# Layer 2's routed rows return inside the program of the blocks: Pool sums the pairs, and layer 3's values follow the last block on TensorE

## The reference, cut to what matters

```python
def _L2_ffn_ref(x, w12, w3, shared_w1, shared_w2, shared_w3, router_w, expert_bias):
    shared = jax.nn.silu(xf @ shared_w1.T) * (xf @ shared_w2.T) @ shared_w3.T
    scores = jax.nn.sigmoid(xf @ router_w.T)
    _, top_idx = jax.lax.top_k(scores + expert_bias, TOP_K)
...
    h = jax.nn.silu(h1) * h2 * gates[:, :, None]
    routed = jnp.einsum('teh,edh->td', h, w3)
    return (shared + routed).reshape(b, s, d)

def _L3_xattn_ref(hidden_states, hidden_states_multi, Wg, Wq, Wk, Wv, Wo, W1, b1, W2, b2):
...
    v = jnp.einsum('bsh,hd->bsd', xm, Wv)
    attn = jax.nn.softmax(jnp.einsum('bqd,bkd->bqk', q, k) * scale, axis=-1)
    e0 = jnp.einsum('bqk,bkd->bqd', attn, v) @ Wo
...
x = x + _L2_ffn_ref(_layernorm(x, axis=-1), ...)
x = x + _L3_xattn_ref(_layernorm(x, axis=-1), ctx_1024, ...)
```

## Time and profile before

| what | value |
|---|---|
| median of 3 runs | 1523.82 us (1521.71 to 1527.78) |
| the profiled execution | 1522.15 us, span of its trace 1520.2 us |
| TensorE busy | 1398.9 us, 92% of the span |
| VectorE, ScalarE, Pool busy | 896.2, 692.9, 355.8 us |
| mean granted clock of TensorE | 0.949 |

### The profile page before, as it was taken

How to read it: one execution, slowest core, us unless ns; L and a number is a source line. 1 busy time by engine, 2 the same in 40 slices (tenths; PEclk the granted TensorE clock), 3 DMA queues, 4 the chain that set the end, 5 groups by cost and what they waited for, 6 DMA issues and landing times. The chain is left out here.

```text
span 1520.2 us, 24680 instructions
## 1 busy us (share of the span) xinstructions
PE 1398.9 (92%) x8362; PEld 1123.9 (74%) x8362; DVE 896.2 (59%) x1703; ACT 692.9 (46%) x1133; POOL 355.8 (23%) x367
## 2 busy tenths in 40 slices
PE   5799999799999999999999699999989888996894
PEld 4544444588888889888888677888867776885783
DVE  6778887745555455555545753444455657654555
ACT  5356667343443344344333265555543254452431
POOL 2102223311222122122211022333310046531100
PEclk8889999889999999999999899999999979998896
DMA  6802120111111111111110024555521143332000
GB/s 224 258 8 58 47 70 16 55 38 62 41 41 59 44 41 41 62 41 41 53 50 7 20 69 104 142 145 144 139 84 70 42 130 125 111 98 76 29 1 28
DMA packets 63799, 110.83 MB, mean 73 GB/s; under 512 B 10331, under 2 KB 39517, under 8 KB 62845
## 3 DMA queue, kind: packets, MB, share of 16 engines
q1 hardware_dynamic: 61869, 104.93, 23.4%
q0 software_dynamic: 1872, 5.13, 0.9%
HBM read 90.91 MB, written 18.97 MB: 72 GB/s over the span
## 5 line engine op out<-in xcount | busy, mean ns | idle before, releaser
L1217 DVE TENSOR_TENSOR hidden_l<-silu_l,up_l 128x512 f32<-128x512 f32 x128 | 88.0, 688 | 220.3 <-ACT silu_l L1157 220.3
L1157 ACT ACTIVATE silu_l<-gate_l 128x512 f32<-128x512 f32 x128 | 76.5, 598 | 308.6 <-PE up_l L75 308.6
L851 DVE TENSOR_REDUCE maxima<-a_scores 128x1 f32<-128x512 f32 x256 | 164.6, 686 | 41.5 <-PE a_scores L790 40.1
L818 ACT ACTIVATE probs<-b_scores 128x1024 f32<-128x1024 f32 x128 | 131.0, 1023 | 67.1 <-PE b_scores L747 65.1
L75 PE MATMUL out_l<-dn_hi_l,h_lo_l 128*128 128x256 f32 x512 | 144.9, 283 | 0.0
L74 PE MATMUL out_l<-dn_lo_l,h_hi_l 128*128 128x256 f32 x512 | 144.9, 283 | 0.0
L73 PE MATMUL out_l<-dn_hi_l,h_hi_l 128*128 128x256 f32 x512 | 144.7, 283 | 0.0
L1189 POOL TENSOR_TENSOR gu_lo_l<-gu_raw_l,gu_hi_l 128x1024 fp32r<-128x1024 f32 x31 | 74.2, 2393 | 299.1 <-ACT gu_hi_l L1149 299.1
L1241 DVE SCALAR_TENSOR_TENSOR x_sb<-out_l,cw,x_sb 128x256 f32<-128x256 f32 x256 | 109.0, 477 | 22.4 <-PE out_l L75 18.1
L1223 DVE TENSOR_TENSOR h_lo_l<-hidden_l,h_hi_l 128x512 fp32r<-128x512 f32 x128 | 102.2, 798 | 3.2
L73 PE MATMUL gate_l<-xnT_hi_n,gu_hi_l 128*128 128x512 f32 x256 | 101.3, 396 | 1.0 <-DVE xnT_lo_n L191 1.0
(11 more groups left out here) (487 smaller groups left out, 3564.1 us busy)
## 6 DMA issues: line engine op xcount, KB each, us to landing
gu_raw_l<-w_units SPq DMA_DIRECT2D x32, 512.0 KB, 3.7
spread_l<-cw_rows SPq DMA_DIRECT2D x64, 256.0 KB, 3.9
dn_raw_l<-w_units SPq DMA_DIRECT2D x32, 256.0 KB, 2.6
k_stack<-k_stacks SPq DMA_DIRECT2D x8, 768.0 KB, 5.7
staged_l<-w_experts SPq DMA_DIRECT2D x24, 256.0 KB, 2.7
up_raw_l<-w SPq DMA_DIRECT2D x40, 128.5 KB, 3.4
dn_raw_l<-w SPq DMA_DIRECT2D x40, 128.0 KB, 2.0
phi_a<-fside SPq DMA_DIRECT2D x8, 512.0 KB, 3.3
```

The source lines that it names most:

```text
L818: act.activation(probs[u % 4][:, :, :], b_scores[:, u % 2, :, :], ACT.Exp, scale=SCALE).then_inc(exp_done, 1)
L851: dve.tensor_reduce(maxima[k // 16][:, i // 2, i % 2:i % 2 + 1], a_scores[:, k % 2, :], X, ALU.max).then_inc(a_read, 1)
L1157: act.activation(silu[:, q % 2, :], gate[:, q % 2, :], ACT.Silu).then_inc(silu_done, 1)
L1217: dve.tensor_tensor(hidden[:, q % 2, :], silu[:, q % 2, :], up[:, q % 2, :], ALU.mult).then_inc(hidden_done, 1)
```

## The change

The program `l2_return_phase` is gone, and its work stands at the end of `l2_sparse_phase`, ahead of that program's one barrier.

- TensorE's list goes on behind the last block with `wvo` and the eight value tiles. `wvo` lies in bank 0 of `gate`; the value tiles use eight places in PSUM that the blocks and the shared expert used (`value_banks`), with a wait for the last block's result ahead of the seventh tile.
- The halves of `wvo` go into `dn_hi` and `dn_lo`, two instructions of 128x256 for one of 128x512, on ScalarE and on VectorE.
- SyncE waits for the blocks' loads to be used up and for all scatters, then loads the four pairs into buffers that are free by then (`staged`, `gu_raw`, `hidden`, `dn_raw`). `dn_raw` becomes one buffer of two halves for that.
- Pool sums the pairs, behind its last scatter. VectorE only adds the sum to `g.x`; a round takes the statistics of the chunks before.

```diff
-        gu_raw, dn_raw = several("gu_raw", [P, 2, KC, FS]), several("dn_raw", [P, D])
+        gu_raw, dn_raw = several("gu_raw", [P, 2, KC, FS]), sb("dn_raw", [P, 2, D])
...
+        spare = [staged[i][:, :, :] for i in range(RING)]
...
+        parts = [spare[2 * i:2 * i + 2] for i in range(PIECE)]
+        wvo = gate[:, 0, :]
+        value_banks = [gate[:, 1, :], up[:, 0, :], up[:, 1, :], banks[:, 0, :], banks[:, 1, :], gate[:, 0, :], banks[:, 2, :], banks[:, 3, :]]
...
             def _(sp):
...
+                sp.wait_ge(pair_split, 2)
+                for i in range(OUTS):
+                    sp.wait_ge(scattered[i], 16 * len(range(i, NB2, OUTS)))
+                for i in range(PIECE):
+                    for w in range(2):
+                        at = w * T + 2 * i * P
+                        sp.dma_start(parts[i][w], g.routed[at:at + 2 * P, :].rearrange("(c p) e -> p c e", p=P)).then_inc(part_loaded[i], 16)
...
             def _(pe):
...
+                pe.wait_ge(pair_split, 2)
+                pe.wait_ge(x_hi_done, NB2)
+                pe.wait_ge(x_lo_done, NB2)
+                for c in range(KC):
...
+                last.then_inc(wvo_done, 1)
+                pe.wait_ge(wvo_hi_done, KC)
+                pe.wait_ge(wvo_lo_done, KC)
...
+                for m in range(VALUES):
+                    if m == 6:
+                        pe.wait_ge(result_done, NB2)
...
             def _(act):
...
+                act.wait_ge(wvo_done, 1)
+                for k in range(KC):
+                    act.activation(dn_hi[k][:, :], wvo[:, k * D:(k + 1) * D], ACT.Copy).then_inc(wvo_hi_done, 1)
...
             def _(pool):
...
+                for i in range(PIECE):
+                    pool.wait_ge(part_loaded[i], 32)
+                    pool.tensor_tensor(parts[i][0], parts[i][0], parts[i][1], ALU.add).then_inc(summed, 1)
+                    pool.wait_ge(summed, i + 1)
...
             def _(dve):
...
+                for m in range(VALUES - LATE):
+                    value_low(m)
+                for i in range(PIECE):
+                    add_routed(i)
+                    if i >= 1:
+                        take_stats(dve, g, (2 * i - 2, 2 * i - 1))
+                    value_low(VALUES - LATE + i)
+                    dve.wait_ge(returned, i + 1)
+                take_stats(dve, g, (TC - 2, TC - 1))
...
-        l2_return_phase(nc, g)
```

More of the change, by code:

```diff
@@ L2170, in l2_sparse_phase, with v_of @@
         g.pair_hi, g.pair_lo = [g.v_hi[:, 8 + 4 * i:12 + 4 * i, :].rearrange("p (w k) f -> p w k f", w=2) for i in range(2)]
-        g.scattered2 = [(scattered[i], 16 * len(range(i, NB2, OUTS))) for i in range(OUTS)]
+        PIECE, VALUES = TC // 2, CT // P // 2
+        spare = [staged[i][:, :, :] for i in range(RING)]
+        spare += [gu_raw[i][:, :, :, :].rearrange("p w k f -> p (w k f)").rearrange("p (c e) -> p c e", c=2) for i in range(2)]
+        spare += [hidden[:, i, :].rearrange("p (c e) -> p c e", c=2) for i in range(2)] + [dn_raw[:, :, :]]
+        parts = [spare[2 * i:2 * i + 2] for i in range(PIECE)]
+        part_loaded, summed, returned = [sem(f"part_loaded{i}") for i in range(PIECE)], sem("parts_summed"), sem("parts_added")
+        wvo = gate[:, 0, :]
+        value_banks = [gate[:, 1, :], up[:, 0, :], up[:, 1, :], banks[:, 0, :], banks[:, 1, :], gate[:, 0, :], banks[:, 2, :], banks[:, 3, :]]
+        wvo_done, wvo_hi_done, wvo_lo_done = sem("wvo3_done"), sem("wvo3_hi_done"), sem("wvo3_lo_done")
+        values_done, v_hi_done, v_lo_done = sem("v3_done"), sem("v3_hi_done"), sem("v3_lo_done")
+        def v_of(half, m):
+            return half[:, 2 * m:2 * m + 2, :].rearrange("p c e -> p (c e)")
         pair_loaded, pair_split = sem("pair_loaded"), sem("pair_split")
@@ L2342, in _ @@
                         block_down(step - 3, experts.pop(step - 3))
+                pe.wait_ge(pair_split, 2)
+                pe.wait_ge(x_hi_done, NB2)
+                pe.wait_ge(x_lo_done, NB2)
+                for c in range(KC):
+                    f = slice(c * P, (c + 1) * P)
+                    for k in range(KC):
+                        last = mm3(pe, wvo[:, c * D:(c + 1) * D], (g.pair_hi[:, 0, k, f], g.pair_lo[:, 0, k, f]),
+                                   (g.pair_hi[:, 1, k, :], g.pair_lo[:, 1, k, :]), c == 0 and k == 0, k == KC - 1)
+                last.then_inc(wvo_done, 1)
+                pe.wait_ge(wvo_hi_done, KC)
+                pe.wait_ge(wvo_lo_done, KC)
+                pe.wait_ge(b_silu_done, NB2)
+                pe.wait_ge(b_hidden_done, NB2)
+                for m in range(VALUES):
+                    if m == 6:
+                        pe.wait_ge(result_done, NB2)
+                    for j in range(2):
+                        t = slice((2 * m + j) * P, (2 * m + j + 1) * P)
+                        for k in range(KC):
+                            last = mm3(pe, value_banks[m][:, j * D:(j + 1) * D], (g.ctxT_hi[:, k, t], g.ctxT_lo[:, k, t]),
+                                       (dn_hi[k][:, :], dn_lo[k][:, :]), j == 0 and k == 0, k == KC - 1)
+                    last.then_inc(values_done, 1)
             @block.scalar
@@ L2355, in split_dn @@
                         act.wait_ge(down_done, 2 * (n - DEPTH + 1))
[L2356 removed]
+                    act.activation(dn_hi[n % DEPTH][:, :], dn_raw[:, n % DEPTH, :], ACT.Copy).then_inc(dn_hi_done, 1)
                 def split_piece(i):
@@ L2421, in _ @@
                         act.activation(result[b % OUTS], y_bank[b % 2][:, 0:D], ACT.Copy, scale=s.weight[:, b:b + 1]).then_inc(result_done, 1)
+                act.wait_ge(wvo_done, 1)
+                for k in range(KC):
+                    act.activation(dn_hi[k][:, :], wvo[:, k * D:(k + 1) * D], ACT.Copy).then_inc(wvo_hi_done, 1)
+                for m in range(VALUES):
+                    act.wait_ge(values_done, m + 1)
+                    act.activation(v_of(g.v_hi, m), value_banks[m], ACT.Copy).then_inc(v_hi_done, 1)
             @block.gpsimd
@@ L2541, in _ @@
                         dve.tensor_tensor(flat(b_lo[b % 2]), h_bank[b % 2][:, 0:D], f32(flat(b_hi[b % 2])), ALU.subtract).then_inc(b_lo_done, 1)
[L2544 to L2604, removed]
-                    dve.wait_ge(v_hi_done, m + 1)
[L2606 to L2614, removed]
@@ L2623, in _ @@
[L2623 to L2627, removed]
-                for i in range(PIECE):
[L2629 to L2632, removed]
+                    dve.tensor_tensor(g.x[:, chunks, :], g.x[:, chunks, :], parts[i][0], ALU.add).then_inc(returned, 1)
@@ new lines, in _ @@
+                for k in range(KC):
+                    dve.wait_ge(wvo_hi_done, KC)
+                    dve.tensor_tensor(dn_lo[k][:, :], wvo[:, k * D:(k + 1) * D], f32(dn_hi[k][:, :]), ALU.subtract).then_inc(wvo_lo_done, 1)
+                LATE = PIECE
+                for m in range(VALUES - LATE):
+                    value_low(m)
+                for i in range(PIECE):
+                    add_routed(i)
[3 more added lines that the diff above has]
+                    dve.wait_ge(returned, i + 1)
```

14 lines of the change are left out of this document (8 added, 6 removed).

## The result

The changed kernel takes 1515.2 us (median of 5 runs, 1512.4 to 1518.34) against 1523.82: a ratio of 0.9942, 95% interval 0.9924 to 0.996. In a second comparison (first experiment) it was 1511.28 against 1523.48, 0.9914, interval 0.9899 to 0.9929. It is faster, by 6 to 15 us. Runs of one kernel differ by up to 6 (the change) and 8 us (before), so what each part is worth is read from one stretch of the traces, from the last block to the last statistics, which repeats within 0.6 us.

A forecast was written before the change was run, and what follows sets the result against it. In the stretch, a barrier waiting for Pool's DRAIN bounds first, then TensorE, then VectorE. Terms -6.0 - 1.3 + 0.1 - 1.95 - 1.7 = -10.85 us gave 1511.3 or 1513.0, stated as 1512.0; range 1509 to 1517.

The forecast's parts named there:

- The barrier goes: Ahead of `wvo` on TensorE: it starts at 1375.5 instead of 1381.52, behind the last block's matmuls, saving 6.0 us.
- The clock: `wvo` on TensorE: matmuls at 2.4 GHz take 1.42 us and a tail of 0.2 instead of 2.9, saving 1.3.
- Both rivals on the clock behind `wvo`: Clock falls in the gap and returns: 1513.4 us, chance 0.09; stays low for all eight value tiles: 1520.3, chance 0.05.
- Halves in two pieces: `wvo`'s halves on ScalarE and VectorE: two 128x256 instructions each instead of one 128x512, costing 0.1 us, at worst 0.33.
- First four value tiles: From first value matmul until VectorE reaches its first routed work: 7.1 us instead of 9.05, saving 1.95.
- VectorE's loop: VectorE's four rounds without the sums: 7.7 us undisturbed, 8.7 with held-up adds, instead of 10.41, saving 1.7.
- The 1.0 for the lock: VectorE's first three routed adds each meet a running Pool sum on the shared port, together 1.0 us later.
- the rival without that: VectorE's routed adds are not held up or loads come sooner: 1.0 us more saved, 1510.3 to 1512, chance 0.09.
- Ready?: Pairs land at about 1383, 1385, 1387 and 1389, so each Pool sum is there before VectorE wants it.
- What is left at the end: Barrier behind VectorE's last statistics: Pool's DRAIN adds 0 us, and layer 3's front starts at the same clock.
- a sign that it is wrong: Listed sign against the forecast: layer 3's front takes longer than before.
- Slower, by the clock of layer 3's front: Clock recovery in layer 3's front slips: by 11 us all saving is gone, by 20 us 1531; chance 0.04.

The follow-up runs named there:

- first experiment: The changed kernel and the kernel before, both unaltered, run once more: 1511.28 us against 1523.48, ratio 0.9914; stretch 19.89 us against 30.21.
- two experiments: Kernel before with pairs' sums moved to Pool, barrier kept: loop 7.71 us, ratio 0.9982. Changed kernel loading pairs from input x: loop 7.72 us, ratio 0.9927.
- second profile: Profile of the unaltered changed kernel's repeat run: stretch 19.89 us, VectorE's loop 9.38, layer 3's front 30.5; ratio to the kernel before 0.9914.
- pairs from the input: Changed kernel, but SyncE loads the eight pieces from input x without waiting for the scatters, leaving routed rows out: stretch 18.23 us, ratio 0.9927.

## Why the prediction was right, and which terms were off

The forecast of 1512.0, faster, with 1509 to 1517, holds both medians, 1515.2 and 1511.28, and the mechanism is the one described. That the second median comes so near is in part chance: it lies 12.2 us below the kernel before, and the stretch accounts for 9.7 to 10.3. By its steps, with the first profile of after:

- *The barrier goes*, -6.0: right. No wait ahead of `wvo`.
- *The clock*, -1.3: right. `wvo` to its copy took 1.64 for 1.62 forecast, at 1.00, and the pause of 1.58 ahead of the values left the clock up. Both rivals on the clock behind `wvo` are out.
- *Halves in two pieces*, +0.1: from copy to first value 1.55 instead of 1.47.
- *First four value tiles*: 7.3 instead of the 7.1 forecast.
- *VectorE's loop*, -1.7: **the step that was mis-sized.** It gave 0.6 and 1.0 in the two profiles. The 7.7 us for an undisturbed loop were right to 0.02 (two experiments). The 1.0 for the lock was as measured, 1.09, though it came from one add held up fully, not three by parts; in every profile of this kernel one add is held up, so the rival without that is out. What failed is "Ready?": "I put the pairs at about 1383, 1385, 1387 and 1389". SyncE's load came 2.6 us behind the last scatter for 2.8 forecast, but the first pair was there 4.9 us behind that load (4.3 in the second profile), not 3.2. I had taken the shortest of the eight landings, 2.7, and an issue; but a pair is two loads, and behind the old barrier too the first was there only after 3.8 and the second after 6.25 (the run with Pool's sums in the kernel before). The landings themselves did not get slower: the median of the eight is 4.5 and 4.6 in the two profiles, 5.0 before. In the first profile the issue of the first pair was 0.9 longer, so its second pair came after 7.1, against 6.2 in the second profile. What lengthened that issue, and why the first pair took 4.3 and not 3.8 in the second profile, was not tried. So VectorE waits 0.88 for the second sum, and 0.43 in the second profile.
- *What is left at the end*: the DRAIN "I take 0, by the 47 ns" was wrong, since the program of that row issues no DMA on Pool. It takes 3.24 us, from 1393.1 to 1396.3, and costs nothing only because VectorE ends 0.9 later; in the forecast's own times it would have ended some 0.8 ahead of VectorE (1390.3 + 0.2 + 3.2 against 1394.5, an estimate). So the sum stands, but not for the reason given. "I take the same start" of the front: it took as long in one profile, and 1.3 us longer in the other, which the prediction had named as a sign that it is wrong.
- *Slower, by the clock of layer 3's front*: the front was 1.3 longer at most, not 11. The clock came back 8.4 to 8.5 us behind the barrier in the two profiles of before, 8.3 and 11.5 us in those of the change; the front with 11.5 is the one with the later weights, so how much of the 1.3 is the clock stays open.

The sum, -10.85, measured -9.7 and -10.3; by steps, in the first profile, -6.15 - 1.29 + 0.08 - 1.76 - 0.60 = -9.72.

The rule of the Trainium skill on the shared port (SBUF — State Buffer, section on the two separate sides) said that Pool would wait for adds as well, which no row of before showed: the third sum's 1.76 shows it. The other rule of the Trainium skill, which gives elementwise adds to VectorE (GPSIMD Engine Reference, Engine selection), leads to the version without Pool's sums. The prediction put that at 9.2; it measured 9.2 to 9.3, and Pool's sums still brought 0.5 to 1.0.

## What to carry to other kernels

A barrier behind DMAs that Pool issued can cost more than the transfers (here Pool's DRAIN ended 4.2 us behind the start of the last scatter, while SyncE could load the scattered rows 2.6 us behind it), so move work across it that needs none of them, and count the DMAs. Work moved to Pool was worth its full time, 2.7 us, only where it was done before VectorE's adds of two SBUF operands began; where they met, late sums and held-up adds left 0.5 to 1.0 of it. And a step that needs two loads comes with the later of them, so price it by the median landing, not by the shortest.

## What the runs showed of the hardware

- Pool's DRAIN at the end of a program took 40 ns and 82 to 89 ns more for each DMA that Pool had issued in it: 129, 701 and 3235 ns for 1, 8 and 39. They were 3235 whether the DRAIN began 6.6 us behind the last scatter's start (pairs from the input) or 14.5 (the change).
- Pool's two-operand instruction held up VectorE's normalisation too, which reads one tensor: 4.54 us instead of 2.67 beside 2.34 us of Pool. The Trainium skill (SBUF — State Buffer, Who interferes with whom) names such operations among those that can take the shared port, and this agrees. The statistics beside a sum kept their 0.74 to 0.75.
- The stretch began between 1374.1 and 1383.1 us from the span's start in the fourteen profiles, behind code that is nearly the same in all of them. Why was not tried.
